# Linear attention: key-value sums and outputs head by head on column and row tiles of the TensorE array, the second half's q spread between the first half's outputs

## Chip, cores and metric

The kernel runs on one core of one Trainium2 chip. The metric is the device time of one execution in microseconds (us); lower is better. The traces come from the hardware profiler. TensorE (PE), VectorE (DVE), ScalarE (ACT), GpSimd (POOL) and the DMA queues issued from SyncE (SP) run side by side and wait for one another by semaphores.

## The reference, cut to what matters

Two transformer layers run in sequence. Only the first stage, the linear attention of layer 0, is touched. Its input is `x` (2 x 1024 x 512), with 16 heads of 32 features:

```
q = elu(x Wq^T) + 1 ;  k = elu(x Wk^T) + 1 ;  v = x Wv^T          (per head)
kv  = einsum('bhtd,bhte->bhde', k, v)                               32 x 32 per head
z   = 1 / (einsum('bhtd,bhd->bht', q, k.sum(axis=t)) + 1e-06)
out = einsum('bhtd,bhde,bht->bhte', q, kv, z) ;  y = out Wo^T
then layernorm(x + y)
```

After it come a feed-forward with fp4 weights, a gated linear attention and a routed feed-forward. None of them is changed.

## The kernel before

**Tiling.** `linear_attention` works on one batch row after the other (`b` = 0, 1). Each has 1024 tokens: eight token tiles of 128 (`NT` = 8) in two halves of 512 (`TB` = 4 tiles each, `h` = 0, 1). The 512 features are four groups `g` of 128, each with four heads of 32 (`DH` = 32, `HG` = 4). Every large product is done as three matmuls with 512 moving columns (`three_products`, lines 41 to 43: high times high, high times low, low times high), so one product of 128 x 512 with a contraction over 512 is 12 matmuls.

**The steps on TensorE.** `tile_kv(b, n)` projects k and v of a token tile (24 matmuls). `add_kv(b, n)` adds that tile's k^T v into PSUM: one fp32 matmul for each group `g`, with all 128 features of the group as weights and its 128 v columns and a column of ones as moving data; the trace shows each fp32 matmul as two records (line 647). So 4 x 4 heads are multiplied and only the four diagonal blocks of 32 x 32 are wanted. `query(b, h, m)` projects group `m` of a half's q (12 matmuls). `numerators(b, t)` multiplies q with the masked sums, one fp32 matmul for each group, again two records (line 675). `transpose_att` turns the result (four transposes, line 686), and `project_out(b, t)` multiplies with Wo (12 matmuls).

**The steps on the other engines.** ACT takes exponentials (`key_exp`, `query_exp`), copies v (`value`), makes the high parts (`att_high`, `x_high`) and unpacks feed-forward weights (`values`). DVE finishes k and q (`keys`, `queries`), masks the key-value sums with `head_mask` (`sums`, four instructions on lines 465 and 467), divides (`attend`, five instructions on lines 478 to 482), makes the low parts (`att_low`, `x_low`), adds the residual and takes the statistics (`finish`), and normalises (`normalise`). POOL takes the square root's inverse.

**What sets the order.** Each engine's order is written out by hand, in the loops at the end of its function. On TensorE a batch row runs: eight times `tile_kv` and `add_kv`, with `query(b, 0, 0)` ahead of the last `add_kv`; the first half's q; then the outputs of tiles 0 to 3 with `numerators`, `transpose_att`, `project_out`; in it the second half's four `query` calls in one run; then the outputs of tiles 4 to 7. In batch row 1, `transpose_rows` for the next stage stands there too. ACT copies the feed-forward scales (line 376) after `x_high(1)`, ahead of the second tile's `key_exp`. PSUM has eight banks: the sums in banks 0 and 1 (`KV0`), which `project_out` uses later (`YP`); q and the transposes in banks 2 and 3 (`QP`, `TP`); k, v and the numerators in banks 4 to 7 (`PROJ`). The second half's q goes into the same tile `q` as the first half's, so DVE may write it only when the first half's numerators are done (`s_num`).

Of the kernel before, what the change touches and what calls it, by code (L numbers as in the profile page):

```python
# [7 lines left out]
F32 = mybir.dt.float32  # L8
# [141 lines left out]
def linear_attention(nc, x_in, xT, wT, gu_packed, gu_scales, dn_packed, carried, const):  # L150
# [5 lines left out]

    ctx, sems = ExitStack(), []
    ctx.callback(clear_semaphores, nc, sems)
    with ctx:
# [20 lines left out]
        kvz = put("a_kvz", [P, KC, P + HG], 200)  # L180
# [3 lines left out]
        v1 = [put(f"a_v1_{i}", [P, KC, P + 1], 24 + i * 65 / 32) for i in range(2)]  # L184
# [12 lines left out]
        KV0, YP, QP, TP, PROJ, FG = 0, 0, 2, 2, 4, 4  # L197
# [116 lines left out]
        def _(act):  # L314
            def x_high(n):
                act.wait_ge(s_xt[n], 16)
                if n >= 2:
                    act.wait_ge(s_q, KC * (n - 1))
                cols = slice(P, BLK) if n == 0 else slice(0, BLK)
                act.activation(xt_hi[n % 2][:, :, cols], xt_raw[n % 2][:, :, cols], ACT.Copy).then_inc(s_xth, 1)  # L320
# [17 lines left out]
            def value(b, n):  # L338
# [3 lines left out]
                act.activation(v1[n % 2][:, :, 0:P], ps[:, PROJ + 2 * (n % 2) + 1, :].rearrange("p (g e) -> p g e", g=KC),  # L342
                               ACT.Copy).then_inc(s_vr, 1)

            def query_exp(b, h, m):
# [4 lines left out]
                act.activation(e[:, :], ps[:, QP + m % 2, :], ACT.Exp).then_inc(s_eq, 1)  # L350
# [9 lines left out]
            for i in (WK, WV):  # L360
                for c in range(KC):
                    act.wait_ge(s_kvw[i][c], 16)
                    act.activation(w_hi[i][:, c, :], w_raw[i][:, c, :], ACT.Copy).then_inc(s_wh[i], 1)
            x_high(0)
            unpacked = {1: (0, 1), 2: (2,), 3: (3, 4), 4: (5, 6, 7), 5: (8, 9), 6: (10, 11, 12), 7: (13, 14, 15)}
            for b in range(NB):
                for n in range(NT):
# [20 lines left out]
                for m in range(KC):  # L388
# [6 lines left out]
                    elif b and m == 0:  # L395
                        values(NCHUNK - 1)
                if b == 0:
                    values(20)
                    values(21)
                for t in range(3):  # L400
                    att_high(b, t)
                query_exp(b, 1, 0)
# [5 lines left out]
                query_exp(b, 1, 1)  # L408
                if b == 0:
                    x_high(2)  # L410
                query_exp(b, 1, 2)
                query_exp(b, 1, 3)
# [4 lines left out]
        def _(dve):  # L417
# [8 lines left out]
            def x_low(n):  # L426
                dve.wait_ge(s_xth, n + 1)
                cols = slice(P, BLK) if n == 0 else slice(0, BLK)
# [14 lines left out]
            def keys(b, n):  # L443
# [3 lines left out]
                dve.wait_ge(s_kvt, max(0, i - 1))  # L447
                dve.scalar_tensor_tensor(out=k[n % 2][:, :], in0=ps[:, PROJ + 2 * (n % 2), :], scalar=0.0, in1=e[:, :],
                                         op0=ALU.max, op1=ALU.add).then_inc(s_k, 1)

            def queries(b, h, m):
# [3 lines left out]
                dve.wait_ge(s_num, NT * b + TB * h)  # L455
                dve.scalar_tensor_tensor(out=q[:, m, :], in0=ps[:, QP + m % 2, :], scalar=0.0, in1=e[:, :],
                                         op0=ALU.max, op1=ALU.add).then_inc(s_qr, 1)

            def sums(b):
                dve.wait_ge(const.ready, 1)  # L460
                dve.wait_ge(s_kvt, NT * (b + 1))
                dve.wait_ge(s_num, NT * b)
                kvp = ps[:, KV0:KV0 + 2, 0:2 * (P + 1)].rearrange("p a (g e) -> p a g e", g=2)
                for a in range(2):
                    dve.tensor_tensor(kvz[:, 2 * a:2 * a + 2, 0:P], kvp[:, a, :, 0:P],
                                      const.head_mask[:, :].unsqueeze(1).to_broadcast([P, 2, P]), ALU.mult)
                    ins = dve.tensor_tensor(kvz[:, 2 * a:2 * a + 2, P:P + HG],
                                            kvp[:, a, :, P:P + 1].to_broadcast([P, 2, HG]),
                                            const.head_mask[:, 0:P:DH].unsqueeze(1).to_broadcast([P, 2, HG]), ALU.mult)
                ins.then_inc(s_kv, 1)  # L470

            def attend(b, t):
                i = NT * b + t
                num = ps[:, PROJ + 2 * (t % 2):PROJ + 2 * (t % 2) + 2, 0:2 * (P + HG)].rearrange("p a (g e) -> p a g e", g=2)
                dve.wait_ge(s_num, i + 1)
                dve.wait_ge(s_tp, max(0, i - 1))
                for a in range(2):
# [1958 lines left out]
```

## Time and profile before

| what | value |
|---|---|
| median of 3 runs | 1035.98 us (1033.57 to 1036.64) |
| profiled execution | 1035.46 us, of which the span on the core is 1033.7 us |
| mean granted TensorE clock | 0.967 |
| TensorE busy | 942.8 us, 91% of the span |
| DVE, ACT, POOL busy | 671.2 us, 402.6 us, 305.0 us |
| the next stage's first matmul starts at | 244.19 us |

The page gives busy time by engine; the timeline gives starts. A matmul record of 512 columns is shown 0.39 us long while the next one starts 0.23 us after it, since ends are modelled; so the distance of two starts is what a matmul takes on TensorE. The number in brackets at the end of a row is the idle time ahead of it, and the arrow names what ended it.

### The profile page before, as it was taken

The page shows a single profiled execution, that of the slowest core. Times are in us where ns is not written, and L with a number is a line of the kernel's source. Part 1 is how long each engine was busy: PE and PEld are TensorE (multiplying, and loading weights), DVE is VectorE, ACT ScalarE, POOL GpSimd, SP SyncE. Part 2 cuts the span into 40 slices and gives each one's busy share as a digit, 9 for nine tenths or more (in the row PEclk, how much of TensorE's full clock was granted, in tenths as well). Part 3 has the DMA queues.
Part 4 walks back from the last instruction along what each step waited for, and adds up shares of the span by engine and source line. Part 5 has one row for each costly group of instructions (what it writes and reads, how often), then busy time and mean ns, then how long its engine had stood idle before and what let it go on. Part 6 is the DMA issues. An engine that isn't in the chain of part 4 may idle for free.

```text
span 1033.7 us, 12330 instructions
## 1 busy us (share of the span) xinstructions
PE 942.8 (91%) x4182; PEld 739.7 (72%) x4182; DVE 671.2 (65%) x1317; ACT 402.6 (39%) x673; POOL 305.0 (30%) x269
## 2 busy tenths in 40 slices
PE   7999999897899999999998988999989789989992
PEld 5777888775577877777766666777857568778882
DVE  4766653677988688688667666657684686463052
ACT  4532122212334543543564564454543263313220
POOL 1000100002576444344333222131224321734332
PEclk9999999999899999999999988999989899989997
DMA  8432100202000000000100110010200343250030
GB/s 285 133 107 87 42 31 31 73 11 57 16 16 11 0 1 1 1 1 1 41 1 1 51 42 1 1 41 1 82 1 22 122 154 110 76 180 11 31 123 41
DMA packets 41790, 52.63 MB, mean 51 GB/s; under 512 B 5888, under 2 KB 23680, under 8 KB 41728
## 3 DMA queue, kind: packets, MB, share of 16 engines
q1 hardware_dynamic: 39904, 47.63, 14.3%
q0 software_dynamic: 1824, 4.22, 1.2%
q8 instruction: 34, 0.56, 0.2%
q14 instruction: 28, 0.23, 0.1%
HBM read 41.33 MB, written 10.50 MB: 50 GB/s over the span
## 4 chain that ended last, share of the span: by engine, by line
PE 44%; DVE 15%; issue 8%; ACT 5%; POOL 3%; DMA 1%; DVEq 0%; ACTq 0%; POOLq 0%
PE ps_gla L41 11%; PE ps_gla L42 10%; PE ps_gla L43 10%; DVE acc L1528 7%; PE ps_gla L2059 5%; PE ps_gla L2060 4%; ACT acc L1255 1%; DVE router_junk L1664 1%; PE ps_gla L2163 1%; POOL p_lo L1898 1%; DVE gsg L1626 1%; PE ps_gla L2094 1%; PE ps_gla L2149 1%; DMA gw_raw<-in_gla_woT 1%; DVE junk L1696 1%
## 5 line engine op out<-in xcount | busy, mean ns | idle before, releaser
L1528 DVE SCALAR_TENSOR_TENSOR acc<-ps_gla,gu_scale,acc 128x512 f32<-128x512 f32 x264 | 196.2, 749 | 66.6 <-ACT acc L1255 45.1
L2059 PE MATMUL ps_gla<-xt_hi,gu_val 128*128 128x512 f32 x352 | 146.9, 417 | 19.3 <-DVE acc L1528 8.5
L2060 PE MATMUL ps_gla<-xt_lo,gu_val 128*128 128x512 f32 x352 | 139.8, 397 | 0.0
L2059 PEld LDWEIGHTS ps_gla<-xt_hi,gu_val 128*128 128x128 f32 x352 | 67.1, 191 | 59.7 <-DVE acc L1528 41.4
L1255 ACT ACTIVATE acc<-ps_gla,gu_scale 128x512 f32<-128x512 f32 x88 | 60.5, 688 | 119.0 <-PE ps_gla L2060 119.0
L1970 POOL TENSOR_TENSOR fsg<-fsg,acc 128x512 f32<-128x512 f32 x44 | 62.1, 1410 | 132.2 <-DVE acc L1528 132.2
L616 POOL TENSOR_TENSOR a_rstd<-a_var,minus_half 128x1 f32<-128x1 f32 x16 | 10.8, 677 | 227.2 <-DVE a_var L508 227.2
L2060 PEld LDWEIGHTS ps_gla<-xt_lo,gu_val 128*128 128x128 f32 x352 | 67.5, 192 | 11.0
L1975 POOL TENSOR_TENSOR fh_lo<-fsg,fh_hi 128x512 fp32r<-128x512 f32 x44 | 56.8, 1291 | 51.9 <-ACT fh_hi L1267 51.9
L41 PE MATMUL ps_gla<-dn_hi,fh_hi 128*128 128x512 f32 x176 | 70.5, 401 | 1.6 <-POOL fh_lo L1975 1.6
L42 PE MATMUL ps_gla<-dn_hi,fh_lo 128*128 128x512 f32 x176 | 69.6, 396 | 0.0
L43 PE MATMUL ps_gla<-dn_lo,fh_hi 128*128 128x512 f32 x176 | 69.4, 394 | 0.0
L2026 POOL TENSOR_TENSOR mh_lo<-mh,mh_hi 128x512 fp32r<-128x512 f32 x32 | 42.7, 1335 | 89.8 <-ACT mh_hi L1487 89.7
L1482 ACT ACTIVATE mh<-ps_gla,b_sb 128x512 f32<-128x512 f32 x32 | 22.0, 689 | 100.0 <-PE ps_gla L43 92.2
L41 PE MATMUL ps_attn<-a_w_hi,xt_hi 128*128 128x512 f32 x128 | 52.4, 410 | 7.3 <-DVE a_w_lo L527 6.1
L41 PE MATMUL ps_gla<-mw_hi,mh_hi 128*128 128x512 f32 x128 | 51.2, 400 | 5.4 <-issue 4.1
L42 PE MATMUL ps_attn<-a_w_hi,xt_lo 128*128 128x512 f32 x128 | 50.9, 398 | 0.0
L43 PE MATMUL ps_attn<-a_w_lo,xt_hi 128*128 128x512 f32 x128 | 50.8, 397 | 0.0
L42 PE MATMUL ps_gla<-mw_hi,mh_lo 128*128 128x512 f32 x128 | 50.8, 397 | 0.0
L43 PE MATMUL ps_gla<-mw_lo,mh_hi 128*128 128x512 f32 x128 | 50.8, 397 | 0.0
L41 PE MATMUL ps_gla<-mxt_hi,mw_hi 128*128 128x512 f32 x128 | 49.8, 389 | 0.0
L42 PE MATMUL ps_gla<-mxt_hi,mw_lo 128*128 128x512 f32 x128 | 49.8, 389 | 0.0
(267 smaller groups left out, 2229.4 us busy)
## 6 DMA issues: line engine op xcount, KB each, us to landing
mw_raw<-in_w SPq DMA_DIRECT2D x16, 512.0 KB, 3.8
a_nib<-in_gate_up_packed SPq DMA_DIRECT2D x88, 64.0 KB, 2.2
x<-x SPq DMA_DIRECT2D x16, 256.0 KB, 2.5
mw_raw<-x SPq DMA_DIRECT2D x8, 512.0 KB, 4.2
out<-mw_raw SPq DMA_DIRECT2D x8, 512.0 KB, 2.9
xt_raw<-in_xT SPq DMA_DIRECT2D x3, 1024.0 KB, 5.0
x<-in_x SPq DMA_DIRECT2D x3, 1024.0 KB, 6.0
a_nib<-in_down_packed SPq DMA_DIRECT2D x8, 256.0 KB, 3.1
```

The lines of the kernel that those rows point to most:

```text
L41: pe.matmul(out, lh, rh, start=first, stop=False)
L42: pe.matmul(out, ll, rh, start=False, stop=False)
L43: return pe.matmul(out, lh, rl, start=False, stop=last)
L616: pool.tensor_tensor(rstd[i % 2][:, :], var[i % 2][:, :], const.minus_half[:, 0:1], ALU.pow).then_inc(s_rstd, 1)
L1255: act.activation(acc[part][u // 2 % 2][:, :], ps[:, FG, :], ACT.Copy, scale=gu_scale[:, part * IT + j, 0:1]).then_inc(s_g0, 1)
L1482: act.activation(h[j % 2][:, :], ps[:, H + j % 4, :], ACT.Gelu_apprx_tanh, bias=b1_sb[:, j:j + 1]).then_inc(m_g, 1)
L1528: dve.scalar_tensor_tensor(out=a[:, :], in0=ps[:, FG + c, :], scalar=gu_scale[:, part * IT + j, c:c + 1], in1=a[:, :], op0=ALU.mult, op1=A ...
L1970: pool.tensor_tensor(f_sg[k % 2][:, :], f_sg[k % 2][:, :], acc[1][k % 2][:, :], ALU.mult).then_inc(s_h, 1)
L1975: pool.tensor_tensor(f_lo[k % HS][:, :], f_sg[k % 2][:, :], f_hi[k % HS][:, :].bitcast(F32), ALU.subtract).then_inc(s_hl, 1)
L2026: pool.tensor_tensor(h_lo[j % HS][:, :], h[j % 2][:, :], h_hi[j % HS][:, :].bitcast(F32), ALU.subtract).then_inc(m_hl, 1)
L2059: pe.matmul(ps[:, FG + c, :], gu_val[:, o, c, :], xt_hi[b % 2][:, c, :], start=True, stop=False)
L2060: pe.matmul(ps[:, FG + c, :], gu_val[:, o, c, :], xt_lo[b % 2][:, c, :], start=False, stop=True).then_inc(s_gu, 1)
```

## The change

**Head by head.** `add_kv` is 16 matmuls instead of 4: for each head the 32 k columns are the weights and the 32 v columns with a column of ones are moving data, and the result lies on 32 PSUM partitions. The four heads of a group stand on four column tiles of the array (128 rows x 32 columns each). `numerators` is now called for two token tiles at once and is 32 matmuls: for each head, weights of 32 rows x 128 tokens and 33 moving columns, on four row tiles, each with a PSUM bank of its own. The mask is gone: `sums` is one copy, `attend` is three instructions instead of five.

**Order.** The second half's q calls are spread: one ahead of `numerators` of tiles 0 and 1, one behind, one ahead of tiles 2 and 3, one behind `transpose_att` of tile 3. Its first two groups go to a new tile `q_next`, so that DVE can write them while the numerators of the first half are still to come. PSUM banks are dealt out anew (`Q_BANK`, `Y_BANK`); the sums take one bank. `transpose_att(0, 7)` moves ahead of `tile_kv(1, 0)`. On DVE and ACT `queries`, `query_exp`, `attend`, `att_low`, `finish` move in step.

**At the start.** The second token tile's columns of `x` are split into high and low parts on their own, ahead of the other two tiles. The copy of the feed-forward scales moves on ACT from behind the first `value` to behind the sixth.

```diff
+        q_next = [put(f"a_q_next{b}", [P, 2, BLK], (20, 108)[b]) for b in range(NB)]
-        KV0, YP, QP, TP, PROJ, FG = 0, 0, 2, 2, 4, 4
+        KV, TP, PROJ, FG = 0, 2, 4, 4
+        Q_BANK = ((2, 3, 2, 3), (2, 1, 0, 1))
+        Y_BANK = (1, 0, 0, 1, 0, 1, 0, 1)
...
+            act.wait_ge(s_xt[0], 16)
+            act.activation(xt_hi[0][:, :, P:2 * P], xt_raw[0][:, :, P:2 * P], ACT.Copy).then_inc(s_x0h, 1)
             x_high(0)
...
                             x_high(1)
-                            act.wait_ge(s_gs, 16)
-                            act.activation(gu_scale[:, :, :], gu_scale16[:, :, :], ACT.Copy).then_inc(s_gsc, 1)
...
+                        elif n == 5:
+                            act.wait_ge(s_gs, 16)
+                            act.activation(gu_scale[:, :, :], gu_scale16[:, :, :], ACT.Copy).then_inc(s_gsc, 1)
...
             def sums(b):
-                for a in range(2):
-                    dve.tensor_tensor(kvz[:, 2 * a:2 * a + 2, 0:P], kvp[:, a, :, 0:P],
-                                      const.head_mask[:, :].unsqueeze(1).to_broadcast([P, 2, P]), ALU.mult)
...
+                dve.tensor_copy(kvz[:, :, :], ps[:, KV, 0:KC * (DH + 1)].rearrange("p (g e) -> p g e", g=KC)).then_inc(s_kv, 1)
...
-                if b or n:
+                if i == 1:
+                    pe.wait_ge(s_x0l, 2)
+                elif i:
                     pe.wait_ge(s_xtl, 2 * b + h + 1)
...
                 for g in range(KC):
-                    ins = pe.matmul(ps[:, KV0 + g // 2, (g % 2) * (P + 1):(g % 2 + 1) * (P + 1)], k[n % 2][:, g * P:(g + 1) * P],
-                                    v1[n % 2][:, g, :], start=(n == 0 and g % 2 == 0), stop=(n == NT - 1), skip_group_check=True)
+                    for j in range(HG):
+                        h = HG * g + j
+                        ins = pe.matmul(ps[j * DH:(j + 1) * DH, KV, g * (DH + 1):(g + 1) * (DH + 1)], k[n % 2][:, h * DH:(h + 1) * DH],
+                                        v1[n % 2][:, h, :], start=(n == 0 and g == 0), stop=(n == NT - 1), skip_group_check=True)
...
-                for g in range(KC):
-                    ins = pe.matmul(ps[:, PROJ + 2 * (t % 2) + g // 2, (g % 2) * (P + HG):(g % 2 + 1) * (P + HG)],
-                                    q[:, g, col:col + P], kvz[:, g, :], start=True, stop=True)
-                ins.then_inc(s_num, 1)
+                for u in (t, t + 1):
+                    for g in range(KC):
+                        for j in range(HG):
+                            d = slice(j * DH, (j + 1) * DH)
+                            ins = pe.matmul(ps[:, PROJ + j, num_col(u, g)], query_out(b, h, g)[d, (u % TB) * P:(u % TB + 1) * P], kvz[d, g, :],
+                                            start=True, stop=True)
+                    ins.then_inc(s_num, 1)
...
+                query(b, 1, 0)
                 numerators(b, 0)
-                numerators(b, 1)
+                query(b, 1, 1)
                 transpose_att(b, 0)
+                transpose_att(b, 1)
+                query(b, 1, 2)
                 numerators(b, 2)
-                transpose_att(b, 1)
                 project_out(b, 0)
-                numerators(b, 3)
+                project_out(b, 1)
                 transpose_att(b, 2)
-                project_out(b, 1)
-                query(b, 1, 0)
                 transpose_att(b, 3)
...
-                for m in range(1, KC):
-                    query(b, 1, m)
+                query(b, 1, 3)
                 project_out(b, 2)
                 numerators(b, 4)
                 project_out(b, 3)
```

On TensorE, between the projections of a token tile (lines 41 to 43) stands `add_kv`; the difference around the second one:

```order
 L42 MATMUL ps_attn<-a_w_hi_62,xt_lo_55 128x512
 L43 MATMUL ps_attn<-a_w_lo_66,xt_hi_53 128x512
-L647 MATMUL ps_attn<-a_v_1_90,a_k_88 128x129 x4
+L666 MATMUL ps_attn<-a_v_1_92,a_k_88 32x33 x16
 L41 MATMUL ps_attn<-a_w_hi_61,xt_hi_53 128x512
 L42 MATMUL ps_attn<-a_w_hi_61,xt_lo_55 128x512
```

Four matmuls of 128 x 129 became sixteen of 32 x 33, at the same place.

TensorE before, behind the last of the first half's q in batch row 0 (`a_att_74` and `a_att_75` are the two buffers of `attend`, `a_at_hi_76` goes into `project_out`):

```order
257 L675 MATMUL ps_attn<-a_kvz,a_q 128x132 [waits a_v_ready,a_q_ready,a_k_ready,a_kv_masked]
258 L675 MATMUL ps_attn<-a_kvz,a_q 128x132 x3
259 L675 MATMUL ps_attn<-a_kvz,a_q 128x132 [waits a_v_ready,a_q_ready,a_k_ready,a_kv_masked]
260 L675 MATMUL ps_attn<-a_kvz,a_q 128x132 x3
261 L686 MATMUL ps_attn<-ident,a_att_74 128x128 [waits a_att_lo_done,a_q_ready,const_ready,a_att_ready]
262 L686 MATMUL ps_attn<-ident,a_att_74 128x128 x3
263 L675 MATMUL ps_attn<-a_kvz,a_q 128x132 [waits a_q_ready,a_att_ready]
```

and the same place in the changed kernel, where `xt_hi_54` and `a_w_hi_63` belong to the second half's q; each line of "..." stands for eleven more matmuls of a `query` call or the rest of a group:

```order
257 L41 MATMUL ps_attn<-xt_hi_54,a_w_hi_63 128x512 [waits a_q_ready,a_w_lo_done2]
...
269 L707 MATMUL ps_attn<-a_kvz,a_q 128x33 [waits a_att_ready,a_v_ready,a_q_ready,a_k_ready,a_kv_masked]
270 L707 MATMUL ps_attn<-a_kvz,a_q 128x33 x31
271 L41 MATMUL ps_attn<-xt_hi_54,a_w_hi_63 128x512 [waits a_residual_added,a_w_lo_done2]
...
283 L720 MATMUL ps_attn<-ident,a_att_74 128x128 [waits a_q_ready,const_ready,a_att_ready]
...
287 L41 MATMUL ps_attn<-xt_hi_54,a_w_hi_63 128x512 [waits a_kv_masked,a_w_lo_done2]
...
299 L707 MATMUL ps_attn<-a_kvz,a_q 128x33 [waits a_q_ready,a_att_ready]
```

A `query` call now stands ahead of the first numerators, one ahead of the first transposes and one ahead of the second numerators.

ACT near the start, before:

```order
7 L342 ACTIVATE a_v_0_89<-ps_attn 128x4x128
8 L320 ACTIVATE xt_hi_54<-xt_raw_58 128x2048
9 L376 ACTIVATE gu_scale<-a_gu_scale_91 128x88
10 L336 ACTIVATE a_e<-ps_attn 128x512
11 L342 ACTIVATE a_v_1_90<-ps_attn 128x4x128
```

and changed:

```order
5 L379 ACTIVATE xt_hi_53<-xt_raw_57 128x4x128
6 L334 ACTIVATE xt_hi_53<-xt_raw_57 128x4x256
7 L350 ACTIVATE a_e<-ps_attn 128x512
8 L356 ACTIVATE a_v_0_91<-ps_attn 128x16x32
9 L334 ACTIVATE xt_hi_54<-xt_raw_58 128x2048
10 L350 ACTIVATE a_e<-ps_attn 128x512
```

The copy of the scales no longer stands ahead of the second tile's exponential, and the first block of `x` is split in two pieces.

## Rows read from the trace of the kernel before

**Rows 1.** The page, part 1: busy time and share of each engine

```profile
PE 942.8 (91%) x4182; PEld 739.7 (72%) x4182; DVE 671.2 (65%) x1317; ACT 402.6 (39%) x673; POOL 305.0 (30%) x269
```

**Rows 2.** Timeline, TensorE: attention's waits; start, length, engine, line, count [idle before]

```profile
16.09 0.47 PE L41 MATMUL ps_attn<-a_w_hi,xt_hi 128*128 128x512 f32 x1 [1.16 <-DVE xt_lo L429]
...
30.16 1.16 PE L647 MATMUL ps_attn<-a_v,a_k 128*128 128x129 f32 x8 [2.04 <-DVE a_k L448]
...
76.91 3.62 PE L675 MATMUL ps_attn<-a_kvz,a_q 128*128 128x132 f32 x16 [2.02 <-DVE a_q L456]
...
94.96 0.47 PE L41 MATMUL ps_attn<-xt_hi,a_w_hi 128*128 128x512 f32 x1 [2.12 <-DVE a_at_lo L493]
...
113.36 0.66 PE L686 MATMUL ps_attn<-ident,a_att 128*128 128x128 f32 x4 [1.36 <-DVE a_att L482]
...
190.61 2.04 PE L675 MATMUL ps_attn<-a_kvz,a_q 128*128 128x132 f32 x16 [1.97 <-DVE a_q L456]
...
193.15 0.66 PE L686 MATMUL ps_attn<-ident,a_att 128*128 128x128 f32 x4 [0.51 <-DVE a_att L482]
...
207.66 0.47 PE L41 MATMUL ps_attn<-xt_hi,a_w_hi 128*128 128x512 f32 x1 [0.38 <-DVE a_at_lo L493]
...
226.03 0.66 PE L686 MATMUL ps_attn<-ident,a_att 128*128 128x128 f32 x4 [1.36 <-DVE a_att L482]
```

**Rows 3.** Timeline: the start of the next stage on TensorE

```profile
244.19 0.56 PE L2059 MATMUL ps_gla<-xt_hi,gu_val 128*128 128x512 f32 x1 [4.52 <-PEq L71]
```

**Rows 4.** Windows, 76 to 94 us: length, TensorE busy, granted clock, DMA

```profile
76.00:94.00 18.00, 15.93 (x84) 0.91 0.46 146
```

**Rows 5.** Timeline: ACT and DVE around the wait for the feed-forward scales

```profile
28.16 0.28 ACT L376 ACTIVATE gu_scale<-a_gu_scale 128x88 f32<-128x88 f16 x1 [9.05 <-DMA a_gu_scale<-in_gate_up_scales]
...
28.95 0.43 DVE L446 TENSOR_SCALAR a_e<-a_e 128x512 f32<-128x512 f32 x1 [10.24 <-ACT a_e L336]
```

**Rows 6.** Timeline, TensorE: the first `add_kv` between projections

```profile
21.39 0.39 PE L43 MATMUL ps_attn<-a_w_lo,xt_hi 128*128 128x512 f32 x1
21.61 1.05 PE L647 MATMUL ps_attn<-a_v,a_k 128*128 128x129 f32 x8
22.42 0.48 PE L41 MATMUL ps_attn<-a_w_hi,xt_hi 128*128 128x512 f32 x1
22.74 0.40 PE L42 MATMUL ps_attn<-a_w_hi,xt_lo 128*128 128x512 f32 x1
22.97 0.39 PE L43 MATMUL ps_attn<-a_w_lo,xt_hi 128*128 128x512 f32 x1
```

**Rows 7.** Timeline, TensorE in a later stage: fp32 records with one moving column

```profile
545.12 0.95 PE L2128 MATMUL ps_gla<-ones,soft 128*128 128x1 f32 x8
545.93 0.49 PE L41 MATMUL ps_gla<-dn_hi,fh_hi 128*128 128x512 f32 x1
546.25 0.40 PE L42 MATMUL ps_gla<-dn_hi,fh_lo 128*128 128x512 f32 x1
```

**Rows 8.** Timeline, a later stage: a matmul on 64 rows (L2156) between whole-array ones

```profile
586.14 1.02 PE L2149 MATMUL ps_gla<-x,k_end 128*128 128x512 f32 x2
...
586.57 0.59 PE L2149 MATMUL ps_gla<-x,k_end 128*128 128x512 f32 x1
...
587.10 0.29 PEld L2156 LDWEIGHTS ps_gla<-pair_t 64*128 64x128 f32 x2 [0.76 <-issue]
587.10 0.49 PE L2156 MATMUL ps_gla<-pair_t 64*128 64x128 f32 x2
...
587.51 0.19 PEld L41 LDWEIGHTS ps_gla<-xt_hi,gw_hi 128*128 128x128 f32 x1
...
587.85 0.40 PE L42 MATMUL ps_gla<-xt_hi,gw_lo 128*128 128x512 f32 x1
```

**Rows 9.** Groups by line, 0 to 260 us: count, busy, mean ns, idle before

```profile
L482 DVE TENSOR_TENSOR a_att<-ps_attn,a_zi 128x256 f32<-128x256 f32 x32 | 12.1, 418 | 0.6
L429 DVE TENSOR_TENSOR xt_lo<-xt_raw,xt_hi 128x2048 fp32r<-128x2048 f32 x3 | 6.9, 2286 | 0.7 <-ACT xt_hi L320 0.7
```

More of the change, by code:

```diff
@@ L183, in linear_attention @@
         k = [put(f"a_k{i}", [P, C], 20 + 2 * i) for i in range(2)]
-        v1 = [put(f"a_v1_{i}", [P, KC, P + 1], 24 + i * 65 / 32) for i in range(2)]
+        q_next = [put(f"a_q_next{b}", [P, 2, BLK], (20, 108)[b]) for b in range(NB)]
+        v1 = [put(f"a_v1_{i}", [P, HEADS, DH + 1], 24 + i * 66 / 32) for i in range(2)]
         gu_scale16 = put("a_gu_scale16", [P, 2 * IT, KC], 29, F16)
@@ L196, in linear_attention, with num_col, query_out @@
         ps = ctx.enter_context(nc.psum_tensor("ps_attn", [P, 8, 512], F32))
-        KV0, YP, QP, TP, PROJ, FG = 0, 0, 2, 2, 4, 4
+        KV, TP, PROJ, FG = 0, 2, 4, 4
+        Q_BANK = ((2, 3, 2, 3), (2, 1, 0, 1))
+        Y_BANK = (1, 0, 0, 1, 0, 1, 0, 1)
+        def num_col(t, g):
+            first = 256 * (t % 2) + g * (DH + 1)
+            return slice(first, first + DH + 1)
+        def query_out(b, h, m):
+            return q_next[b][:, m, :] if h and m < 2 else q[:, m, :]
         s_x0 = sem("a_first_xt_loaded")
@@ L349, in query_exp @@
                 act.wait_ge(s_k, NT * (b + 1))
[L350 removed]
+                act.activation(e[:, :], ps[:, Q_BANK[h][m], :], ACT.Exp).then_inc(s_eq, 1)
             def att_high(b, t):
@@ L399, in _ @@
                     values(21)
-                for t in range(3):
-                    att_high(b, t)
-                query_exp(b, 1, 0)
+                att_high(b, 0)
+                att_high(b, 1)
+                query_exp(b, 1, 1)
+                query_exp(b, 1, 2)
+                if b == 0:
+                    x_high(2)
+                att_high(b, 2)
                 att_high(b, 3)
@@ L454, in queries @@
                 done(dve.tensor_scalar(e[:, :], e[:, :], 1.0, None, ALU.min))
-                dve.wait_ge(s_num, NT * b + TB * h)
-                dve.scalar_tensor_tensor(out=q[:, m, :], in0=ps[:, QP + m % 2, :], scalar=0.0, in1=e[:, :],
+                if h and m < 2:
+                    dve.wait_ge(s_kvt, NT * (b + 1))
+                else:
+                    dve.wait_ge(s_num, NT * b + TB * h)
+                dve.scalar_tensor_tensor(out=query_out(b, h, m), in0=ps[:, Q_BANK[h][m], :], scalar=0.0, in1=e[:, :],
@@ L564, in _ @@
                         nibbles(21)
+                queries(b, 1, 0)
                 attend(b, 0)
@@ L567, in _ @@
                 att_low(b, 0)
+                att_low(b, 1)
+                queries(b, 1, 1)
+                queries(b, 1, 2)
                 attend(b, 2)
-                att_low(b, 1)
+                attend(b, 3)
                 finish(b, 0)
-                attend(b, 3)
                 att_low(b, 2)
```

131 lines of the change are left out of this document (67 added, 64 removed).

## The prediction

> **What bounds the kernel now.** I read the page's busy shares first: TensorE is busy 91% of the span, DVE 65% [rows 1]. Then the timeline. The next stage's first matmul is at 244.19 us [rows 3], and every engine crosses the boundary ahead of it together, so the change can act only on those 244 us, and a microsecond gained there is one gained in the whole. Inside it TensorE's own waits: nine, of 0.38 to 2.12 us [rows 2]. Everywhere else one matmul follows the other, so attention's length is TensorE's work plus these nine gaps. The change wants to close the gaps and pays with another form of small matmul. Both sides are sized below, against the profiled execution of 1035.46 us, which lies 0.5 us under the median of 1035.98; I make no correction for that.
>
> **What the gaps are worth.** They sum to 1.16 + 2.04 + 2.02 + 2.12 + 1.36 + 1.97 + 0.51 + 0.38 + 1.36 = 12.9 us [rows 2]. A gap is counted from a modelled end: a matmul is shown 0.39 us long and the next starts 0.23 us after it [rows 6], so each gap is really 0.16 us longer, 1.4 us for nine. Behind the third, the same sixteen numerator records take 3.62 us, and behind the sixth 2.04 us [rows 2]. The granted clock in 76 to 94 us is 0.91 and not 1 [rows 4]: a part of it ran at 1.2 instead of 2.4 GHz, after the wait. That is 1.6 us more. All waits together: 15.9 us.
>
> **Which go, and what is late next.**
> (a) 16.09: the second token tile waited for the low part of three tiles at once. Its own piece is now done first, on ACT and DVE, a third of the work. Before, DVE finished 1.2 us late; two thirds of its 1.8 us of work (4 x 384 columns, against 2.29 us for 2048 [rows 9]) are more than that. Gone, 1.2.
> (b) 30.16: ACT stood 9.05 us on the DMA of the scales with the second tile's exponential queued behind it, and DVE stood 10.24 us on that [rows 5]. The copy now stands behind the sixth tile. Next on ACT is the copy of Wq's high part, which did not wait for a DMA before when it came at 29 us; I take it as there by 22 us. Gone, 2.0.
> (c) 76.91 and 190.61: the numerators waited for the last q to pass ACT and DVE. A `query` call, 12 x 0.228 = 2.7 us, now stands in between, longer than the waits of 2.0. Gone, with the slow clock. What is queued behind it on DVE is one `queries` more, about 1.1 us, ahead of `attend`; the transposes behind wait for that, covered by the next `query`.
> (d) 94.96, 193.15 and 207.66: `transpose_att` and `query` waited for `att_low` and `attend` in a ring of two buffers. Two transposes now stand behind 2.7 us of q, and the second half's q no longer uses the transposes' banks alone. DVE needs about 1.2 us for an `attend` (its product alone 2 x 0.418 [rows 9]; one instruction of 512 now) and has two to do in 2.7 us plus the transposes. Just enough, gone.
> (e) 113.36 and 226.03, in the second half. There is no q left to put between. DVE does `queries`, `x_low(2)` of 2.29 us [rows 9] in batch row 0 or the low parts of the next stage's input in batch row 1, `normalise`, then two `attend`. Laid out with the durations above I find TensorE late by 0.3, 0.1 and 0.7 us in batch row 0, and by 0.9, 0.6 and 0.6 us in batch row 1. So 3.2 us stay.
> Taken out: 15.9 - 3.2 = 12.7 us. That DVE loses a few instructions (four in `sums`, two in each `attend`) is worth nothing of its own: it is what (d) and (e) already use.
>
> **What the small matmuls cost.** One `add_kv` now: from 21.61 to 22.74 less the 0.23 of the projection's own first matmul, 0.90 us for eight records [rows 6]. A record is spaced 0.110 to 0.113 us. Records with one moving column are spaced the same (545.12 to 546.25 less 0.23, over eight: 0.1125) [rows 7]. So the spacing is not set by the moving columns alone; with 128 columns of weights something else takes as long. No row has a record with 32 columns of weights or 32 rows, thirty-three moving, so its spacing r is bounded: from below, four tiles work at once and r is a quarter of what 33 moving columns take, 0.110 x 33/129 / 4 = 0.007; from above, the whole 0.1125. I take r = 0.028 for both kinds: for `add_kv` both sides, weights (32 of 128 columns) and moving (33 of 129), shrink to a quarter; for `numerators` the weights keep 128 columns, and four row tiles load at once. It is nearest to the rows in that it only scales them.
> Entering and leaving a tile shape costs more. In [rows 8] two whole-array records start at 586.14 and 586.57, 0.43 apart, so the second has streamed by 587.00; yet the weights of the matmul on 64 rows are loaded only at 587.10. Its load of 0.11 and two records of 0.10 (128 moving columns) end at 587.42, and the next projection's weights are loaded only at 587.51. So 0.10 us pass empty on entry and 0.09 on exit, and neither first load hides: 0.11 for 128 columns, 0.03 for 32.
> `add_kv`: 0.10 + 0.03 + 32 x 0.028 + 0.09 + 0.11 = 1.21 us against 0.90, so 0.31 more, sixteen times: 5.0 us.
> `numerators` for two tiles: 0.10 + 0.11 + 64 x 0.028 + 0.09 + 0.11 = 2.17 us (with r unrounded at 0.0275) against 1.9 us for sixteen records at 0.1125 and an unhidden load: 0.27 more, eight times: 2.2 us.
> Nothing covers these; TensorE is the path. The transposes are as many as before.
>
> A rule of the Trainium skill bears on r. "TensorE: Matmul & The Clock Gate", Part 1, states that matmuls never start closer than about 25 ns however few columns they have. No row here shows records that short. By it `add_kv` would come to 1.1 us instead of 1.2, and the sum would stand 1 or 2 us lower; my r lies just above it.
>
> **The sum.** 1035.5 - 12.7 + 5.0 + 2.2 = 1030.0 us, 0.6% under the median. In r the cost is 1024 r - 21.1 us for all small matmuls; it eats the whole 12.7 us at r = 0.033. The forecast thus hangs on a number that the trace doesn't hold, and is a narrow one.
>
> **Rival 1: records have a floor, slower.** If issuing a pair of weight load and matmul has a cost of its own, the equal spacing at 129 and at one moving column [rows 6, 7] is what it would look like. At half that spacing, r = 0.056: `add_kv` 2.1 us (+1.2, sixteen times 19.5), `numerators` 4.0 us (+2.1, eight times 16.7); 1035.5 - 12.7 + 36.2 = 1059 us. At the whole spacing, 1117 us. It decides from r = 0.033. For it: four times the instructions, nothing in the trace is closer than 0.1 us. Against it: every row near 0.1 us also has 128 columns to load or stream, which explains it as well.
> The same page, Part 1, gives 62 ns for each matmul where the sequencer decodes it in microcode; that would be this rival with 0.062, some 1065 us by the same formula. No run here shows which decoding is on.
>
> **Rival 2: the row tiles load one after the other.** `add_kv` is as forecast, but `numerators`' 128-column loads stay in series, r = 0.11 there: 0.41 + 64 x 0.11 = 7.45 us, 5.5 more, eight times 44: 1035.5 - 12.7 + 5.0 + 44 = 1072 us. For it: the loads of [rows 7] are in series. Against: they go to the same rows of the array.
>
> **Rival 3: four tiles at once.** r = 0.007: `add_kv` 0.55 us, `numerators` 0.86 us, together 14 us less than before, 1009 us; half the effect gives 1018.
> The Trainium skill, "TensorEngine Tiling (Array Packing)", Key Properties, says that tiles load and multiply in parallel, which is this rival, and that a change of tile shape drains the engine, which [rows 8] bear out with 0.1 us.
>
> **Rival 4: the gaps stay.** The new order closes only half of the 12.7 us because DVE is late at the first transposes, tiles as forecast: 1036 us. For it: DVE got one `queries` more ahead of `attend`. Against: 2.7 us of cover twice.
>
> **Chances.** Forecast 1030: 0.42. Rival 3: 0.10. Rival 1: 0.20. Rival 2: 0.16. Rival 4: 0.12. Faster than the median by over 0.3% (about what a measurement can tell from no change, 3 us) is the forecast and rival 3: 0.52; within it, rival 4: 0.12; slower 0.36. The range leaves out rival 2 and the extreme of rival 3: 1012 to 1060. The forecast's own range, with r from 0.020 to 0.033 and 2 us on the gaps, is 1020 to 1037.
>
> **What would show it.** In the changed profile: sixteen fp32 matmuls of 32 x 33 from their first start to the second projection start behind them less 0.23 us, 1.2 us; thirty-two of 128 x 33, 2.2 us for a pair of token tiles; no wait above 0.5 us on TensorE ahead of the first numerators and at the second tile's projection; the granted clock at 1 in 76 to 94 us; the next stage's first matmul near 238.7 us. If `add_kv` takes over 1.3 us, or `numerators` over 2.6 us, I am wrong on r; if waits of over 5 us in all remain, I am wrong on the order. Everything behind attention should take as long as before.

## The result and the profile after

The changed kernel takes 1018.32 us (median of 4 runs, 1017.87 to 1020.05) against 1036.31 us (4 runs, 1033.57 to 1036.66) for the kernel before beside it: a ratio of 0.9835, 95% interval 0.9815 to 0.9856. That is 18 us or 1.65% faster. I had said 1030.0, 6 us faster. The direction held, and so did the wide range of 1012 to 1060; the forecast's own range, 1020 to 1037, did not, and two thirds of the gain were not in my sum.

First the page, and then the boundary to the next stage, which answers to [rows 3]. The columns of a timeline are start in us, length in us, engine, line, operation, buffers, tile, shapes, count, and in brackets the engine's idle time before it with what ended it.

```profile
span 1016.4 us, 13804 instructions
...
PE 934.5 (92%) x4950; PEld 726.2 (71%) x4950; DVE 666.8 (66%) x1280; ACT 402.0 (40%) x674; POOL 304.6 (30%) x269
```

```profile
226.45 0.47 PE L2093 MATMUL ps_gla<-xt_hi,gu_val 128*128 128x512 f32 x1 [4.66 <-PEq L71]
```

The next stage starts at 226.45 instead of 244.19: 17.7 us earlier. From there to the end the changed kernel needs 1016.4 - 226.45 = 790.0 us, the one before 1033.7 - 244.19 = 789.5. The whole gain lies in attention, none behind it. TensorE has 768 records more (4950 against 4182 in [rows 1]) and is busy 8 us less.

TensorE's waits in attention, grouped (the changed kernel, 0 to 235 us; total us, times, longest):

```profile
PE ps_attn L41 <- DVE a_w_lo L539: 5.9, 1, 5.9
...
PE ps_attn L41 <- issue: 0.6, 2, 0.3
PE ps_attn L41 <- DVE a_q L482: 0.4, 1, 0.4
PE ps_attn L707 <- issue: 0.4, 1, 0.4
```

The first row is the wait for the first weights, which the kernel before has too (6.10 there, 5.90 here). In this profile all nine waits of [rows 2] are gone (a second profile of the same kernel, below, has small rests of two). Four small ones are new, and in the timeline they read:

```profile
63.42 0.47 PE L41 MATMUL ps_attn<-xt_hi,a_w_hi 128*128 128x512 f32 x1 [0.45 <-DVE a_q L482]
...
105.80 0.47 PE L41 MATMUL ps_attn<-a_w_hi,a_at_hi 128*128 128x512 f32 x1 [0.32 <-issue]
...
201.37 0.65 PE L707 MATMUL ps_attn<-a_kvz,a_q_next 32*128 32x33 f32 x16 [0.40 <-issue]
...
212.83 0.47 PE L41 MATMUL ps_attn<-a_w_hi,a_at_hi 128*128 128x512 f32 x1 [0.32 <-issue]
```

They sum to 1.5 us, or 2.1 with the 0.16 for each modelled end. The window of [rows 4], 76 to 94 us, is now busy throughout at a granted clock of 1.00 (columns: length, TensorE busy, clock, DMA share, GB/s):

```profile
76.00:94.00 18.00, 18.00 (x144) 1.00 0.30 96
```

Then the two small matmuls. `add_kv` as in [rows 6], on TensorE and its weight loads:

```profile
19.54 0.39 PE L43 MATMUL ps_attn<-a_w_lo,xt_hi 128*128 128x512 f32 x1
19.86 0.35 PEld L666 LDWEIGHTS ps_attn<-a_v,a_k 128*32 128x32 f32 x32 [0.35 <-issue]
19.86 0.46 PE L666 MATMUL ps_attn<-a_v,a_k 128*32 128x33 f32 x32
20.25 0.50 PE L41 MATMUL ps_attn<-a_w_hi,xt_hi 128*128 128x512 f32 x1
20.58 0.39 PE L42 MATMUL ps_attn<-a_w_hi,xt_lo 128*128 128x512 f32 x1
```

From the end of the projection (19.54 + 0.23 = 19.77) to the start of the next projection's first matmul (20.58 - 0.23 = 20.35) pass 0.58 us, where 0.90 passed before. One record of this kind alone is shown 0.196 us long, so the thirty-two start on average (0.46 - 0.196) / 31 = 0.0085 us apart. A pair of token tiles in `numerators`:

```profile
80.13 0.39 PE L43 MATMUL ps_attn<-xt_lo,a_w_hi 128*128 128x512 f32 x1
80.45 1.99 PE L707 MATMUL ps_attn<-a_kvz,a_q 32*128 32x33 f32 x64
82.37 0.50 PE L41 MATMUL ps_attn<-a_w_hi,a_at_hi 128*128 128x512 f32 x1
82.71 0.40 PE L42 MATMUL ps_attn<-a_w_hi,a_at_lo 128*128 128x512 f32 x1
```

From 80.36 to 82.48: 2.11 us. My estimate for two token tiles before was 1.9; the trace of before has 0.90 for one (105.94 to 106.84), so 1.80. One record is 0.27 us long, so they start (1.99 - 0.27) / 63 = 0.0273 us apart.

**The account.** Waits and the slow clock behind one of them 15.9 - 2.1 = 13.8 less; `add_kv` sixteen times 0.32 = 5.1 less; `numerators` eight times 0.31 = 2.5 more; the first matmul 0.2 earlier. Together -16.6 of the measured -17.7 us; the 1.1 us left I can't place.

### The profile page after: what moved, and what is told of

Same layout as the page of the kernel before. It is cut to its first block, busy times and chain, and to the rows that moved or that the text cites. A ratio compares the mean times of both kernels' runs of the same rounds, so it can differ in the third digit from the quotient of the medians.

```text
span 1016.4 us, 13804 instructions
## 1 busy us (share of the span) xinstructions
PE 934.5 (92%) x4950; PEld 726.2 (71%) x4950; DVE 666.8 (66%) x1280; ACT 402.0 (40%) x674; POOL 304.6 (30%) x269
## 4 chain that ended last, share of the span: by engine, by line
PE 42%; DVE 17%; issue 9%; ACT 5%; POOL 3%; DMA 1%; DVEq 0%; ACTq 0%; POOLq 0%
PE ps_gla L41 10%; PE ps_gla L42 10%; PE ps_gla L43 10%; DVE acc L1562 9%; PE ps_gla L2093 4%; PE ps_gla L2094 4%; ACT acc L1289 1%; DVE router_junk L1698 1%; PE ps_gla L2197 1%; POOL p_lo L1932 1%; DVE gsg L1660 1%; PE ps_gla L2128 1%; PE ps_gla L2183 1%; ACT fjunk L825 1%; DVE junk L1730 1%
```

## The experiments

The experiments ran in four groups, and in each group the kernel before ran on the same chip (1034.94, 1036.05, 1035.16 and 1034.76 us, 9 to 23 runs); every ratio below is to those. "Boundary" is the start of the next stage's first matmul in the profiled execution; the visit of a small matmul is measured as above, from the modelled end of the projection before to the start of the one behind.

**The changed kernel again** (e0_after), to have it beside the others.

> The changed kernel once more, as the neighbour to compare the three others with on one chip: 1018.3 us, the next stage's first matmul at 226.5 us.

1017.59 us, 0.9823 (0.9799 to 0.9847), boundary 227.52. It had three waits that the first profile of the same kernel lacks: 0.44 us for the first weights (at 7.74), and these two.

```profile
15.10 0.47 PE L41 MATMUL ps_attn<-a_w_hi,xt_hi 128*128 128x512 f32 x1 [0.66 <-DVE xt_lo L541]
...
72.99 1.99 PE L707 MATMUL ps_attn<-a_kvz,a_q 32*128 32x33 f32 x64 [0.45 <-DVE a_q L482]
```

They are the waits of steps (a) and (c) of the prediction, smaller than before but not gone in every execution. Two profiles of one kernel differ by 1.1 us at the boundary, and less than that can't be read from one profile.

**`add_kv` back on the whole array** (e1_whole_kv): four matmuls of 128 x 132 instead of sixteen of 32 x 33. DVE takes the wanted blocks out with four copies instead of one; the rest is as changed.

```diff
                 for g in range(KC):
-                    for j in range(HG):
-                        h = HG * g + j
-                        ins = pe.matmul(ps[j * DH:(j + 1) * DH, KV, g * (DH + 1):(g + 1) * (DH + 1)], k[n % 2][:, h * DH:(h + 1) * DH],
-                                        v1[n % 2][:, h, :], start=(n == 0 and g == 0), stop=(n == NT - 1), skip_group_check=True)
+                    ins = pe.matmul(ps[:, KV + g // 2, (g % 2) * W:(g % 2 + 1) * W], k[n % 2][:, g * P:(g + 1) * P],
+                                    v1[n % 2][:, HG * g:HG * (g + 1), :].rearrange("p h e -> p (h e)"), ...
```

> The changed kernel with the key-value sums back on the whole array (4 fp32 matmuls of 128 x 132 per token tile), all else as changed. Theory 1 (the column tiles overlap, add_kv takes 0.58 us instead of 0.90): slower than the changed kernel by 16 x 0.32 = 5.1 us, 1023.4 us. Rival (the column tiles are worth nothing, all of the gain is in the waits): within 1 us of it, 1018 us.

1021.48 us, 0.9863 (0.984 to 0.9886); boundary 231.17, 3.7 later than in e0_after and 4.7 later than in the first profile. TensorE:

```profile
20.48 0.39 PE L43 MATMUL ps_attn<-a_w_lo,xt_hi 128*128 128x512 f32 x1
20.71 1.06 PE L669 MATMUL ps_attn<-a_v,a_k 128*128 128x132 f32 x8
...
21.84 0.40 PE L42 MATMUL ps_attn<-a_w_hi,xt_lo 128*128 128x512 f32 x1
```

The visit is 20.71 to 21.61, 0.90 us, with no gap on entry. So column tiles gain 3.7 to 4.7 us at the boundary (sixteen visits of 0.32 less are 5.1), where my prediction had them lose 5.0. At the medians it is 3.9 us, where the two intervals overlap a little.

**The same sixteen matmuls in another order** (e4_kv_same_tile): the loops exchanged, so that four heads of one column tile follow one another and not four tiles.

```diff
-                for g in range(KC):
-                    for j in range(HG):
+                for j in range(HG):
+                    for g in range(KC):
```

> The changed kernel with the two loops of add_kv exchanged: the four calls (eight records) of one column tile come one after the other, the same sixteen matmuls. Theory 1 (records are 8.5 ns apart because four column tiles work at once): they come 27 ns apart within a tile, 32 x 0.027 = 0.9 us instead of 0.26, so 0.6 us more per token tile, 16 x 0.6 = 9.6 us, 1028 us. Rival (a record of 32 weight columns and 33 moving columns costs 8.5 ns wherever it stands): no change, 1018 us.

1024.59 us, 0.9894 (0.9874 to 0.9913); boundary 232.45, 4.9 to 6.0 later.

```profile
19.45 0.39 PE L43 MATMUL ps_attn<-a_w_lo,xt_hi 128*128 128x512 f32 x1
19.77 0.90 PE L666 MATMUL ps_attn<-a_v,a_k 128*32 128x33 f32 x32
20.60 0.50 PE L41 MATMUL ps_attn<-a_w_hi,xt_hi 128*128 128x512 f32 x1
20.94 0.39 PE L42 MATMUL ps_attn<-a_w_hi,xt_lo 128*128 128x512 f32 x1
```

Work, instructions and buffers are the same; only the neighbour differs, and the mean distance of records goes from 8.5 to (0.90 - 0.196) / 31 = 22.7 ns, the visit from 0.58 to 1.03 us. This is the run that shows the cause: a record of one tile hides behind those of the three others. The 22.7 is itself a mean: the last records of one tile overlap the first of the next. The last five records of the visit, all of one tile, are these:

```profile
20.34 0.32 PE L666 MATMUL ps_attn<-a_v,a_k 128*32 128x33 f32 x5
```

They start (0.32 - 0.196) / 4 = 31 ns apart. My 27.5 ns is nearly what one tile needs alone. A column tile always writes its own 32 partitions of PSUM, so this run doesn't tell whether the array or the way into PSUM makes one tile wait for itself.

**`add_kv` issued twice** (e6_kv_twice): every matmul of it a second time, so that numerator and denominator both are doubled.

```diff
-                for g in range(KC):
-                    for j in range(HG):
...
+                for r in range(2):
+                    for g in range(KC):
+                        for j in range(HG):
...
```

> The changed kernel with the sixteen matmuls of add_kv issued twice over, so that numerator and denominator are both summed twice. Theory 1 (a visit to the column tiles is 0.31 us of entering and leaving and 32 x 0.0085 = 0.27 us of records): 16 x 0.27 = 4.4 us slower than the changed kernel, 1022.5 us. Rival (the 0.58 us are the records' own): 16 x 0.58 = 9.3 us slower, 1027 us.

1020.93 us, 0.9876 (0.9847 to 0.9906); boundary 231.92, 4.4 to 5.5 later.

```profile
25.69 0.39 PE L43 MATMUL ps_attn<-a_w_lo,xt_hi 128*128 128x512 f32 x1
26.01 0.76 PE L667 MATMUL ps_attn<-a_v,a_k 128*32 128x33 f32 x64
26.70 0.50 PE L41 MATMUL ps_attn<-a_w_hi,xt_hi 128*128 128x512 f32 x1
27.04 0.40 PE L42 MATMUL ps_attn<-a_w_hi,xt_lo 128*128 128x512 f32 x1
```

The visit is 25.92 to 26.81, 0.89 us, as thirteen of the sixteen are (the others 0.93 to 1.02). That is 0.31 us for thirty-two records more, so 0.58 - 0.31 = 0.27 us, or 0.31 with the 8.5 ns of above, is what a visit costs apart from its records. I had put 0.33 for entry, exit and the two unhidden loads. That part of the sum was nearly right, and r was wrong.

**`numerators` back on the whole array** (e2_whole_num), with keys and values in a block-diagonal operand (kvz, zero outside the blocks, which DVE fills with four copies): four matmuls of 132 columns for a token tile instead of sixteen of 33.

```diff
                 for u in (t, t + 1):
                     for g in range(KC):
-                        for j in range(HG):
-                            d = slice(j * DH, (j + 1) * DH)
-                            ins = pe.matmul(ps[:, PROJ + j, num_col(u, g)], query_out(b, h, g)[d, (u % TB) * P:(u % TB + 1) * P], kvz[d, g, :],
-                                            start=True, stop=True)
+                        ins = pe.matmul(ps[:, PROJ + 2 * (u % 2) + g // 2, (g % 2) * W:(g % 2 + 1) * W],
+                                        query_out(b, h, g)[:, (u % TB) * P:(u % TB + 1) * P],
+                                        kvz[:, g, :, :].rearrange("p j e -> p (j e)"), start=True, stop=True)
```

> The changed kernel with the numerators back on the whole array (4 fp32 matmuls of 128 x 132 per token tile, block-diagonal sums), the column tiles and the order kept. Theory 1 (row tiles cost 2.1 us for a pair of token tiles against 1.9 us, since each entry and exit leaves 0.2 us empty): faster than the changed kernel by 8 x 0.2 = 1.7 us, 1016.6 us. Rival (row tiles save time as the column tiles do): slower by 2 us or more.

1017.49 us, 0.9831 (0.9805 to 0.9858); boundary 224.47, 2.0 to 3.1 earlier.

```profile
79.91 0.39 PE L43 MATMUL ps_attn<-xt_lo,a_w_hi 128*128 128x512 f32 x1
80.14 1.96 PE L710 MATMUL ps_attn<-a_kvz,a_q 128*128 128x132 f32 x16
81.86 0.48 PE L41 MATMUL ps_attn<-a_w_hi,a_at_hi 128*128 128x512 f32 x1
82.17 0.40 PE L42 MATMUL ps_attn<-a_w_hi,a_at_lo 128*128 128x512 f32 x1
```

80.14 to 81.94 is 1.80 us against 2.11, eight times 2.5 us; the boundary shows it, the whole time (0.1 us less at the median) does not, within its interval. The row tiles of `numerators` gain nothing for this kernel, then, and cost it 2 to 3 us of attention. (`attend` reads its numerators from other banks here, as the whole-array form leaves them.)

**`numerators` in another order** (e5_num_same_tile): the loops exchanged as in e4.

```diff
-                    for g in range(KC):
-                        for j in range(HG):
+                    for j in range(HG):
+                        for g in range(KC):
```

> The changed kernel with the two inner loops of the numerators exchanged: the four calls of one row tile come one after the other. Theory 1 (records are 27 ns apart because the 0.11 us weight loads of four row tiles overlap): they come 0.11 us apart, 64 x 0.083 = 5.3 us more for a pair of token tiles, 8 x 5.3 = 42 us, 1060 us. Rival (27 ns is what a record of 33 moving columns takes): no change, 1018 us.

1057.06 us, 1.0206 (1.019 to 1.0221): slower than the kernel before. Boundary 266.05.

```profile
71.53 5.62 PE L707 MATMUL ps_attn<-a_kvz,a_q 32*128 32x33 f32 x64
```

(5.62 - 0.27) / 63 = 0.085 us a record, but the clock fell within this visit. Windows of this kernel:

```profile
71.00:73.00 2.00, 2.00 (x25) 1.00 0.89 228
75.00:81.00 6.00, 6.00 (x25) 0.50 0.74 251
```

The last two of its eight visits ran at full clock. One of them begins and ends so:

```profile
243.37 0.63 PE L707 MATMUL ps_attn<-a_kvz,a_q_next 32*128 32x33 f32 x4
...
247.15 0.61 PE L707 MATMUL ps_attn<-a_kvz,a_q 32*128 32x33 f32 x4
...
248.03 0.40 PE L42 MATMUL ps_attn<-a_w_hi,a_at_lo 128*128 128x512 f32 x1
```

The sixty-four records start from 243.37 to 247.15 + 0.61 - 0.27 = 247.49, on average 4.12 / 63 = 0.065 us apart. Within the last four, all of one row tile, it is (0.61 - 0.27) / 3 = 0.113, as for whole-array records: there the loads of 128 columns stand in series. In between, records that read `a_q` (the last groups of one tile) alternate with those that read `a_q_next` (the first groups of the next), so two tiles still overlap. My rival 2 (0.11 throughout) is thus about half true for this order, and the order of the changed kernel avoids it. A row tile has a PSUM bank of its own here, so the run doesn't separate the loads from the bank; that the distance is the load's own 0.11 speaks for the loads.

At full clock a visit takes 4.4 to 4.5 us instead of 2.11; eight times the difference is some 19 us. The rest, some 20 of the 38.5 us at the boundary, goes with the clock: the six visits in which it fell take 5.4 to 6.6 us, and projections behind them start 0.43 us apart instead of 0.23. The mean clock of the whole kernel is 0.949 to 0.952 in all four runs, against 0.969 to 0.972 in e0_after. I had expected 42 us from loads in series alone; 39.5 came at the median, near to it by luck, for the loads gave half and the clock the rest.

**The second half's first q back behind the outputs** (e3_q_back).

```diff
-                queries(b, 1, 0)
                 attend(b, 0)
                 attend(b, 1)
+                queries(b, 1, 0)
...
-                query(b, 1, 0)
                 numerators(b, 0)
+                query(b, 1, 0)
```

> The changed kernel with the second half's first q call behind the first numerators again, on TensorE and on VectorE. Theory 1 (that call covers the wait for the last q): the wait of 2.0 us is back ahead of the numerators in both batch rows, 0.16 us more each by the modelled ends, and in batch row 0 the clock falls after it, 1.6 us more: 4.3 to 6 us slower, 1023 to 1024 us. Rival (another q call behind covers the loss, the order is elastic): within 1 us of 1018.

1026.9 us, 0.9918 (0.9898 to 0.9938): 9.3 us more than e0_after, boundary 7.6 later.

```profile
64.94 0.47 PE L41 MATMUL ps_attn<-xt_hi,a_w_hi 128*128 128x512 f32 x1 [1.92 <-DVE a_q L482]
...
72.70 1.99 PE L707 MATMUL ps_attn<-a_kvz,a_q 32*128 32x33 f32 x64 [2.03 <-DVE a_q L482]
...
181.10 1.99 PE L707 MATMUL ps_attn<-a_kvz,a_q 32*128 32x33 f32 x64 [1.97 <-DVE a_q L482]
```

and its windows (clock in the third number behind the stretch):

```profile
68.00:78.00 10.00, 7.97 (x84) 0.83 0.49 151
78.00:94.00 16.00, 16.00 (x134) 1.00 0.33 99
180.00:200.00 20.00, 18.90 (x190) 0.91 0.01 2
```

The two waits of [rows 2] are back at their old size, 2.03 and 1.97, 4.3 us with the modelled ends. The lower clock adds (1 - 0.83) x 10 + (1 - 0.91) x 20 = 3.5 us at most, and the wait at 64.94, which has another cause (below), is 1.5 longer than in the changed kernel. These make 9.3 where 7.6 to 9.3 were measured, so the cover from one `query` call is shown; the 9 us as a whole are not its price alone.

**Only the start of the change, in the kernel before** (b1_start): the second tile's own piece of x first, and the copy of the feed-forward scales behind the sixth tile. **Only the copy** (b3_scales).

```diff
-                cols = slice(P, BLK) if n == 0 else slice(0, BLK)
+                cols = slice(2 * P, BLK) if n == 0 else slice(0, BLK)
...
+            act.wait_ge(s_xt[0], 16)
+            act.activation(xt_hi[0][:, :, P:2 * P], xt_raw[0][:, :, P:2 * P], ACT.Copy).then_inc(s_x0h, 1)
...
-                            act.wait_ge(s_gs, 16)
-                            act.activation(gu_scale[:, :, :], gu_scale16[:, :, :], ACT.Copy).then_inc(s_gsc, 1)
...
+                        elif n == 5:
+                            act.wait_ge(s_gs, 16)
+                            act.activation(gu_scale[:, :, :], gu_scale16[:, :, :], ACT.Copy).then_inc(s_gsc, 1)
```

(b3_scales has the last two pieces only.)

> The kernel before with the two edits at the start alone: the second token tile's columns of x split on their own, the copy of the feed-forward scales moved behind the sixth tile. Theory 1 (both waits lie on the path): 1.2 + 2.0 us and 0.16 us for each, 3.5 us faster than before, 1032.5 us. Rival (TensorE waits later for what it no longer waits for here): within 1 us of before.

> The kernel before with the copy of the feed-forward scales moved behind the sixth tile, alone. Theory 1: the wait of 2.0 us goes, 2.2 us with its modelled end; if the fall of the clock after the wait ahead of the numerators depends on where in time that wait lies, it goes as in the kernel with both edits and 1.6 us more are gained, 1032 us, else 1034 us. Rival: the two edits gain only together, within 1 us of before.

b1_start: 1029.86 us, 0.9952 (0.9938 to 0.9967), boundary 239.11, with the third wait as it was:

```profile
72.75 2.04 PE L682 MATMUL ps_attn<-a_kvz,a_q 128*128 128x132 f32 x16 [2.02 <-DVE a_q L459]
```

Its clock is 1.00 in 68:78, 76:94 and 94:110. b3_scales: 1032.64 us, 0.9979 (0.9966 to 0.9993), boundary 243.36, with the same wait of 2.02 and a clock of 0.89, 0.88 and 0.93 there. Both parts help in whole time, the copy alone by 2 us or so. b1_start gained 6.2 us at the median where 3.5 were due; 3.5 us would be 0.9966, just inside its interval.

**The kernel before once more** (b0_before), for that clock.

> The kernel before once more, for a second profile: is the granted clock in 76 to 94 us 0.91 again (the fall belongs to this order of work) or 1 (it varies from execution to execution)? Theory: 0.91 again, 1036 us. Rival: 1, with a span 1.6 us shorter.

1035.14 us, ratio 1.0007, boundary 243.37. The wait is there, and the clock is not down (76 to 94 us):

```profile
16.44 0.47 PE L41 MATMUL ps_attn<-a_w_hi,xt_hi 128*128 128x512 f32 x1 [2.08 <-DVE xt_lo L429]
...
77.04 2.04 PE L675 MATMUL ps_attn<-a_kvz,a_q 128*128 128x132 f32 x16 [2.02 <-DVE a_q L456]
79.58 0.66 PE L686 MATMUL ps_attn<-ident,a_att 128*128 128x128 f32 x4 [0.51 <-DVE a_att L482]
...
94.08 0.47 PE L41 MATMUL ps_attn<-xt_hi,a_w_hi 128*128 128x512 f32 x1 [2.12 <-DVE a_at_lo L493]
...
76.00:94.00 18.00, 14.29 (x84) 1.00 0.46 147
```

One kernel, one wait, and 0.91 in one execution [rows 4] and 1.00 in another. Two more things are in these rows. A wait of 0.51 stands at 79.58 that [rows 2] don't have: the slow clock had covered it. So from the first numerators to the next q it is 94.08 - 77.04 = 17.04 us here and 94.96 - 76.91 = 18.05 in [rows 2], and the fall cost 1.0 us net, not 1.6. And the second tile's wait, 1.16 in [rows 2], is 2.08 here, 1.77 in b3_scales and 0.31 in b1_start. Against this execution, b1_start's boundary is 4.3 us earlier, of which 1.8 are the second tile's wait and 1.8 the one ahead of the second `add_kv` (1.83 at 30.30 here, none there).

**What bounds attention next** (e7_nib_late). In the changed kernel DVE waits for the DMA of packed feed-forward weights ahead of the second q of the first half:

```profile
61.26 0.49 DVE L460 TENSOR_SCALAR a_nib<-a_nib,shift 128x512 int32<-128x512 int32 x1 [1.62 <-DMA a_nib<-in_gate_up_packed]
```

and TensorE stands 0.45 at 63.42 for it. In e3_q_back this DMA wait is 2.77 us, which makes the 1.92 there. The run moves two unpackings one q later:

```diff
-            masked = {0: (0, 1), 1: (2,), ..., 7: (16, 17)}
+            masked = {0: (0, 1), 1: (2,), ..., 7: (16,)}
...
                         sums(b)
+                        if b == 0:
+                            nibbles(18)
                     elif b == 0 and m == 0:
-                        nibbles(18)
+                        nibbles(17)
```

> The changed kernel with two unpackings of feed-forward weights (tiles 17 and 18) one q later on VectorE, since it stands up to 1.6 us on their DMA there with q queued behind. Theory: the TensorE wait of 0.2 to 0.5 us behind the first q goes, 0.3 to 1 us faster than the changed kernel. Rival: the wait moves to the next q, no change.

1015.6 us, 0.9826 (0.9803 to 0.9849), boundary 227.01, no earlier than the changed kernel's. The wait moved, as the rival said:

```profile
72.56 1.99 PE L709 MATMUL ps_attn<-a_kvz,a_q 32*128 32x33 f32 x64 [1.60 <-DVE a_q L482]
```

**Both of the small gains** (e8_both): e2_whole_num and e7_nib_late in one kernel, their edits unchanged.

> The changed kernel with both edits that looked harmless or better: numerators on the whole array with the column tiles kept, and the two unpackings later. Theory: the gains of each against the changed kernel (0.9 us and 1.7 us of span in their traces) add up, 1015 us. Rival: they don't, since the waits that each leaves are the other's, 1016.5 to 1018 us.

1015.51 us, 0.9821 (0.9795 to 0.9846), boundary 224.31, 2 to 3 us ahead of the changed kernel's. In whole time the ratio lies inside the changed kernel's own interval (0.9799 to 0.9847), so attention is shorter in the trace, and a faster kernel is not shown.

## Why the prediction was right and wrong

**What bounds the kernel, and where the gain can fall:** right. The 17.7 us at the boundary are the whole gain, and the rest took 790.0 against 789.5 us.

**Steps (a) to (d), the waits that go:** right in the main. All are gone in the first profile; e0_after keeps 0.66 us of (a) and 0.45 of (c). For the cover of the first numerators e3_q_back gives the proof, by the waits of 2.03 and 1.97 that return; for (a) and (b) b1_start. No run takes (d) by itself.

**Step (e), what stays in the second half:** too dark. I kept 3.2 us of lateness for DVE at the second half's transposes. No wait there is on DVE; the rows at 105.80, 201.37 and 212.83 are "issue", 0.3 to 0.4 each. In their place came one wait that I hadn't seen, for the packed weights' DMA by way of DVE (0.45). Together 2.1 instead of 3.2 us with the modelled ends.

**The step that failed: r of `add_kv`.** The term "0.10 + 0.03 + 32 x 0.028 + 0.09 + 0.11 = 1.21 us, 0.31 more, sixteen times: 5.0 us" measures 0.58 us, 0.32 less, sixteen times: 5.1 us less. These 10.1 us are most of the 12 by which I missed. Entry and exit were nearly right (0.27 to 0.31 by e6_kv_twice, against 0.33). The r of 27.5 ns was a fourfold scaling of a single tile's streaming: it shrank columns to a quarter and let no tile overlap another. e4_kv_same_tile shows such records, 31 ns apart within one tile and 22.7 in the mean, and the changed order 8.5 ns, near the 7 ns of rival 3, which I had given 0.10. The prediction named only a visit of over 1.3 us as a sign against r, none of a shorter one. I had even used the overlap myself, for the loads of the row tiles, and then not for the column tiles' streaming. Had I carried it through both, the column tiles' r would have been 7 ns, and the sum 1030.0 - 16 x 32 x 0.0205 = 1019.5 us, against 1018.3 measured. Rival 3's line "half the effect gives 1018" came near the measured time by luck: none of its terms gives 1018 (halfway from 1030 to 1009 is 1019.5), and what happened was its whole effect in one kind of visit and none in the other.

**The r of `numerators`:** right, and for the reason given. 27.3 ns measured against 27.5; four loads of 0.11 overlap fourfold, and e5_num_same_tile shows 0.113 within one tile. The whole visit is 2.11 against 2.17 us; as before it was 1.80 and not 1.9, it costs 0.31 and not 0.27 more. Rival 3's 0.86 us for it fell: by these distances the loads set the pace here and not the 33 moving columns.

**The clock term of 1.6 us:** not a property of the wait. b0_before and b1_start have the same wait of 2.02 us and no fall; b3_scales and e3_q_back have it and fall. It belonged to the execution that I read, and its net price there was 1.0 us, since it covered a wait of 0.51. A sum against a median should have given it a chance and not the full size.

**The rivals.** Rival 1 (a floor per record, 56 ns or more) is refuted by 8.5 ns. Rival 2 (row tiles' loads in series) is refuted for this order, and half true for the other: 65 ns at full clock where it had 110, and 1057 us with the fall of the clock. Rival 3 (four tiles at once) is right for `add_kv` alone. Rival 4 (gaps stay) is refuted by the waits.

**The pages.** "TensorE: Matmul & The Clock Gate", Part 1, of the Trainium skill has matmuls never start closer than about 25 ns. The thirty-two records of `add_kv` start 8.5 ns apart on four column tiles, which is 17 ns for a matmul of the program, as each is two records: the measurement disagrees for tiles that take turns, and decides. Within one column tile the records are 31 ns apart, which does not contradict it. In the prediction, 25 ns for r would have lowered the sum by 2.6 us, not by 1 or 2. "TensorEngine Tiling (Array Packing)", Key Properties, of the Trainium skill says that tiles load and multiply in parallel. Both visits agree, and the exchanged loops show how far it depends on the order: with one tile's matmuls in a row, the distance goes from 8.5 to 22.7 ns and from 27.3 to 65, and only where two tiles meet do they still overlap.

**Left open.** Why the clock falls in some executions, and in e5_num_same_tile in all; where 1.1 us of the account are; whether e2, e7 or e8 beat the changed kernel in whole time; whether array or PSUM makes a tile wait for itself.

## What to carry to other kernels

Where small matmuls go to tiles of the array, order them so that neighbours in the program use different tiles. As an estimate from these runs, price a record as the larger of its parts (load, moving columns) divided by the number of tiles that take turns (here 0.11 / 4 = 27 ns and 28 / 4 = 7 ns, against 27.3 and 8.5), plus some 0.3 us for entering and leaving the tile shape. Column tiles paid here, where both load and moving columns shrink (0.90 to 0.58 us); row tiles with full 128-column loads did not (2.11 against 1.80 us on the whole array with a block-diagonal operand). Where TensorE waits for its own last result to come back through ACT and DVE, one call of independent work in between closes the wait (e3_q_back); check that cover against the DMA that the helping engines wait for, which here left 0.45 to 1.60 us.

## What the runs showed of the hardware that I had not expected

- Records of four column tiles start 8.5 ns apart when the tiles take turns, and 22.7 ns when each tile's records stand together (31 ns within a tile); row tiles with 128-column weights 27.3 and, at full clock, 65 ns (113 ns within a tile).
- The granted clock fell with TensorE busy throughout: in e5_num_same_tile it is 1.00 at 71 to 73 us, and 0.50 (1.2 instead of 2.4 GHz) in 75 to 81, from within 5.6 us of numerators whose row tiles don't take turns, with no wait ahead of them.
- The same wait of 2.02 us was followed by a granted clock of 0.91 in one execution of the kernel before, and of 1.00 in another; the fall covered a wait of 0.51 us and cost 1.0 us net.
